# Turning softmax probabilities with a transposing DMA of two float16 parts, in a cross-attention and feed-forward kernel

## What is computed

```python
def block(x, ctx, pos, mask, Wq, Wk, Wv, Wo, kernel, bias):
    h = layernorm(x)
    q = rope((h @ Wq).reshape(32, 64, 32, 128), pos)
    k = rope((ctx @ Wk).reshape(32, 64, 8, 128), pos)
    v = (ctx @ Wv).reshape(32, 64, 8, 128)
    scores = q . k / sqrt(128)            # each k, v head serves 4 q heads
    scores = where(mask == 0, -1e9, scores)
    p = softmax(scores)
    x = x + (p @ v).reshape(32, 64, 4096) @ Wo
    f = layernorm(x)
    return x + f @ mxfp4(kernel) + bias   # kernel rounded to 4-bit values and back
```

## Time and profile before

| | |
|---|---|
| median of three runs | 1138.07 us (1137.52 to 1138.55) |
| span of the profiled execution | 1136.2 us (its own time beside the span is not recorded; the median stands 1.9 us above the span) |
| PE busy | 1126.4 us, 99% |
| DVE, ACT, POOL busy | 810.1, 769.0, 629.6 us |
| DMA | 65.6 MB, mean 58 GB/s |

### The profile page before, as it was taken

The page is one execution under the profiler, slowest core; times in us unless marked ns, Lnnn a source line. Parts: engine busy times, 40 slices in busy tenths (PEclk is TensorE's granted clock), DMA queues, the critical chain, the costliest instruction groups (busy, mean ns, idle before and its releaser), DMA issues.

```text
span 1136.2 us, 19698 instructions
## 1 busy us (share of the span) xinstructions
PE 1126.4 (99%) x6315; PEld 971.5 (86%) x6326; DVE 810.1 (71%) x1753; ACT 769.0 (68%) x2306; POOL 629.6 (55%) x518
## 2 busy tenths in 40 slices
PE   7999999999999999999999999999999999999998
PEld 6888888888888888888888788888888888888886
DVE  7877777777777777688788756656566665656698
ACT  7866676566676766688766566676766677666763
POOL 7854645365554655569666556545654446545433
PEclk9999999999999999999999999999999999999999
DMA  8311211112111111224124421110201112020001
GB/s 260 86 34 43 75 39 46 33 43 66 35 51 33 61 39 37 93 71 142 48 68 111 116 75 43 38 48 20 83 10 29 48 38 65 11 73 20 1 7 69
DMA packets 60196, 65.57 MB, mean 58 GB/s; under 512 B 17216, under 2 KB 36032, under 8 KB 60096
## 3 DMA queue, kind: packets, MB, share of 16 engines
q1 hardware_dynamic: 59184, 61.96, 18.3%
q0 software_dynamic: 768, 2.10, 0.6%
q10 hardware_dynamic: 144, 0.26, 0.1%
HBM read 58.01 MB, written 4.19 MB: 55 GB/s over the span
## 4 chain that ended last, share of the span: by engine, by line
PE 98%; DMA 1%; DVE 0%; POOL 0%; issue 0%; DVEq 0%
PE proj L539 15%; PE proj L540 15%; PE proj L541 15%; PE pS L671 9%; PE pO L725 9%; PE pO L726 9%; PE pO L727 9%; PE pV L703 3%; PE pV L704 3%; PE pO L735 3%; PE pT L686 3%; PE pO L738 1%; PE proj L602 1%; PE proj L595 1%; PE proj L553 1%; DMA t<-table,tiny 1%
## 5 line engine op out<-in xcount | busy, mean ns | idle before, releaser
L915 ACT CAST PS<-pT 64x256 fp32r<-64x256 f32 x256 | 93.8, 367 | 296.9 <-PE pV L704 293.5
L1436 POOL TENSOR_TENSOR t<-t,SIN 128x512 f32<-128x512 f32 x124 | 159.7, 1288 | 185.9 <-ACT t L924 185.5
L539 PE MATMUL proj<-XH,QH 128*128 128x512 f32 x500 | 195.7, 391 | 0.0
L541 PE MATMUL proj<-XH,QL 128*128 128x512 f32 x500 | 194.8, 390 | 0.0
L540 PE MATMUL proj<-XL,QH 128*128 128x512 f32 x500 | 194.7, 389 | 0.0
L725 PE MATMUL pO<-OH,AH 128*128 128x512 f32 x432 | 171.6, 397 | 0.0
L726 PE MATMUL pO<-OL,AH 128*128 128x512 f32 x432 | 169.2, 392 | 0.0
L727 PE MATMUL pO<-OH,AL 128*128 128x512 f32 x432 | 168.5, 390 | 0.0
L1440 POOL TENSOR_TENSOR qT<-qT,t 128x512 f32<-128x512 f32 x124 | 159.8, 1289 | 9.7
L1156 DVE TENSOR_TENSOR qT<-proj,COS 128x512 f32<-128x512 f32 x128 | 88.4, 690 | 95.1 <-PE proj L541 55.5
L1002 ACT ACTIVATE pS<-pS,tiny 128x64 f32<-128x64 f32 x504 | 140.7, 279 | 7.7 <-DVE tiny L1339 3.6
(11 more groups left out here) (216 smaller groups left out, 2581.4 us busy)
## 6 DMA issues: line engine op xcount, KB each, us to landing
QR<-wq SPq DMA_DIRECT2D x64, 256.0 KB, 2.6
OR<-wo SPq DMA_DIRECT2D x62, 256.0 KB, 3.2
CR<-ctxT SPq DMA_DIRECT2D x16, 256.0 KB, 5.1
KR<-wk SPq DMA_DIRECT2D x16, 256.0 KB, 2.6
UR<-wv SPq DMA_DIRECT2D x16, 256.0 KB, 3.9
acc<-x SPq DMA_DIRECT2D x15, 256.0 KB, 3.8
out<-acc SPq DMA_DIRECT2D x15, 256.0 KB, 2.3
rawx<-x SPq DMA_DIRECT2D x8, 256.0 KB, 2.9
```

The lines of the kernel that those rows point to most:

```text
L539: pe.matmul(dst, lh, rh, start=k == 0, stop=False)
L541: made = pe.matmul(dst, ll, rh, start=False, stop=k == last)
L1436: pool.tensor_tensor(t[:, :], t[:, :], SIN[:, 512 * (s % 2):512 * (s % 2) + 512], ALU.mult).then_inc(g_qs, 1)
```

## The change

p is turned by the DMA engines. DVE scales p by 2^14 as well and writes it into PSUM (`sm` is now the lower half of bank pT). ACT casts it to float16 into P16, each 64-column block written twice side by side (the high part, for both halves of the partitions), at the end of its step. DVE writes the rest as float16 into P16's second half, each block once, beside zeros set at the start. SP starts one transposing DMA of the 128x1024 tile into PT16, one step later. One more step on, at the head of their steps, ACT casts the four high blocks back to the matmul format in PS with the scale 2^-14, and POOL does the same with the four low blocks. `values` reads both from PS, in the same number of matmuls and columns. PE's `turn_p` is gone. POOL's ring for its own DMAs is made smaller (4096).

```diff
+P_SCALE = 2.0 ** 14
-        VS, PS = sb("VS", [128, 2, 8, 256], F32R), sb("PS", [128, 2, 256], F32R)
+        VS, PS = sb("VS", [128, 2, 8, 256], F32R), sb("PS", [128, 8, 128], F32R)
-        PL = sb("PL", [128, 2, 256], F32R)
-        sm = sb("sm", [128, 256], F32)
+        P16, PT16 = sb("P16", [128, 1024], FP16), sb("PT16", [128, 8, 128], FP16)
+        sm = pT[:, 0:256]
 SP, after the weight loads of step n, for m = n - 6:
+            def turn_p(m):
+                if m:
+                    sp.wait_ge(a_ps, m)
+                    sp.wait_ge(g_ps, m)
+                sp.wait_ge(a_ph, m + 1)
+                sp.wait_ge(v_pl, m + 1)
+                sp.dma_start(PT16[:, :, :], P16[:, :], transpose=True).then_inc(d_pt, 16)
 PE:
-            def turn_p(m):
-                pe.wait_ge(v_pn, m + 1)
...
-                for hp in range(2):
-                    made = pe.transpose(pT[:, 128 * hp:128 * hp + 128], sm[:, 128 * hp:128 * hp + 128],
-                                        ident[:, :])
-                made.then_inc(e_pt, 1)
             def values(m):
-                pe.wait_ge(v_pl, 2 * m + 2)
-                pe.wait_ge(a_px, 2 * m + 2)
+                pe.wait_ge(a_ps, m + 1)
+                pe.wait_ge(g_ps, m + 1)
...
-                    pe.matmul(pV[:, b], VS[:, b, j, c], PS[:, b, :], start=True, stop=False)
-                    made = pe.matmul(pV[:, b], VS[:, b, j, c], PL[:, b, :], start=False, stop=True)
+                    pe.matmul(dst, VS[:, b, j, c], PS[:, b:4:2], start=True, stop=False)
+                    made = pe.matmul(dst, VS[:, b, j, c], PS[:, 4 + b::2], start=False, stop=True)
 ACT, p_high(m) at the end of step m + 5 and p_turned(m) first in step m + 7:
             def p_high(m):
-                act.wait_ge(e_pt, m + 1)
-                if m:
-                    act.wait_ge(e_pv, m)
-                for i in range(2):
-                    act.copy(PS[ROWS[i], i, :], pT[ROWS[i], 0:256]).then_inc(a_ph, 1)
+                act.wait_ge(v_pn, m + 1)
+                if m:
+                    act.wait_ge(d_pt, 16 * m)
+                act.activation(P16[:, 0:512].rearrange("p (a d k) -> p a d k", a=4, d=2),
+                               sm.rearrange("p (a k) -> p a k", a=4).unsqueeze(2).broadcast_to([128, 4, 2, 64]),
+                               ACT.Copy).then_inc(a_ph, 1)
+            def p_turned(m):
+                act.wait_ge(d_pt, 16 * m + 16)
+                if m:
+                    act.wait_ge(e_pv, m)
+                act.activation(PS[:, 0:4], PT16[:, 0:4], ACT.Copy, scale=1.0 / P_SCALE).then_inc(a_ps, 1)
-                        act.copy(PS[ROWS[1 - i], i, :], PS[ROWS[i], i, :].bitcast(F32)).then_inc(a_px, 1)
 DVE, p_low(m) in step m + 6 right after the sum of the output projection:
-                dve.tensor_tensor(sm.rearrange("p (a k) -> p a k", a=4), v4, rinv.unsqueeze(2).broadcast_to([128, 4, 64]),
-                                  ALU.mult).then_inc(v_pn, 1)
+                dve.scalar_tensor_tensor(sm.rearrange("p (a k) -> p a k", a=4), v4, P_SCALE,
+                                         rinv.unsqueeze(2).broadcast_to([128, 4, 64]), ALU.mult,
+                                         ALU.mult).then_inc(v_pn, 1)
+            def p_low(m):
+                dve.wait_ge(a_ph, m + 1)
+                v = sm.rearrange("p (h i k) -> p h i k", h=2, i=2)
+                high = P16[:, 0:512].rearrange("p (h i d k) -> p h i d k", h=2, i=2, d=2)[:, :, :, 0, :]
+                dve.tensor_tensor(P16[:, 512:1024].rearrange("p (h u k) -> p h u k", h=2, u=4)[:, :, 0:4:3, :],
+                                  v, high, ALU.subtract).then_inc(v_pl, 1)
-                    for i in range(2):
-                        dve.wait_ge(a_ph, 2 * (m - 1) + i + 1)
-                        dve.tensor_tensor(PL[ROWS[i], i, :], pT[ROWS[i], 0:256], PS[ROWS[i], i, :].bitcast(F32),
-                                          ALU.subtract).then_inc(v_pl, 1)
 POOL, first in step m + 7:
+            def p_turned(m):
+                pool.wait_ge(d_pt, 16 * m + 16)
+                if m:
+                    pool.wait_ge(e_pv, m)
+                pool.tensor_scalar(PS[:, 4:8], PT16[:, 4:8], 1.0 / P_SCALE, None, ALU.mult).then_inc(g_ps, 1)
-    nc = _bacc.Bacc("TRN2", target_bir_lowering=False, num_devices=1)
+    nc = _bacc.Bacc("TRN2", target_bir_lowering=False, num_devices=1, dynamic_dma_scratch_size=4096)
```

More of the change, by code:

```diff
@@ L87 @@
 PART = [range(0, 1), range(1, 4), range(4, 8)] + [range(k, k + 1) for k in range(8, QUANT)]
-def quant_steps(n):
-    parts = quant_parts(n)
-    return sum(QUANT * i + PART[c].stop for i, c in parts[-1:]) if parts and parts[-1][1] < len(PART) else (
-        QUANT * parts[-1][0] + QUANT if parts else 0)
 def quant_parts(n):
@@ L494, in _ @@
                     load_stream(streamed(n))
+                if 0 <= n - 6 < PAIRS:
+                    turn_p(n - 6)
                 if n + 1 in X_AT and X_AT[n + 1] >= 8:
@@ L694, in values @@
                 c = slice(128 * (G % 2), 128 * (G % 2) + 128)
-                pe.wait_ge(v_pl, 2 * m + 2)
-                if not m:
-                    pe.wait_ge(v_const, 3)
-                pe.wait_ge(a_px, 2 * m + 2)
+                pe.wait_ge(a_ps, m + 1)
+                pe.wait_ge(g_ps, m + 1)
                 pe.wait_ge(v_vl, v_count(s - 2 * (G % 2), p))
@@ L963, in _ @@
                 m = n - 5
+                if 0 <= m - 2 < PAIRS:
+                    p_turned(m - 2)
                 if 0 <= n - 1 < PAIRS and n - 1 not in ALONE:
@@ L1227, in _ @@
             dve.memset(mhalf, -0.5).then_inc(v_const, 1)
-            for i in range(2):
-                dve.memset(PL[ROWS[1 - i], i, :].bitcast(F32), 0.0).then_inc(v_const, 1)
+            dve.memset(P16[:, 512:1024].bitcast(F32), 0.0).then_inc(v_const, 1)
             statistics("x", 0)
@@ L1284, in _ @@
                         last_sums()
+                if 0 <= m - 1 < PAIRS:
+                    p_low(m - 1)
                 if n in X_AT and X_AT[n] >= 8:
@@ L1356, in _ @@
                     normalise("f", FFN_AT[n])
-                if 0 <= m - 1 < PAIRS:
-                    for i in range(2):
-                        dve.wait_ge(a_ph, 2 * (m - 1) + i + 1)
-                        dve.tensor_tensor(PL[ROWS[i], i, :], pT[ROWS[i], 0:256], PS[ROWS[i], i, :].bitcast(F32),
-                                          ALU.subtract).then_inc(v_pl, 1)
                 if 0 <= m - 2 < PAIRS and n > PAIRS + 1:
@@ L1470, in _ @@
             for n in range(OPENED, END):
+                if 0 <= n - 7 < PAIRS:
+                    p_turned(n - 7)
                 if is_last(n):
```

29 lines of the change are left out of this document (12 added, 17 removed).

## The result

The changed kernel takes **1162.15 us** (median of four runs, 1161.32 to 1162.75) against 1138.07 us before (1137.52 to 1138.55 in four runs): a ratio of **1.0211, 95% interval 1.0199 to 1.0224**. It is 24 us slower, where 3.6 us faster was forecast. The profiled execution has a span of 1159.4 us and a time of 1161.32 us, 1.9 us above its span, as was assumed.

A forecast was written before the change was run, and what follows sets the result against it. PE's instruction stream, 99% busy, was taken to bound the kernel. From 1138.07 us, -29.4 + 1.0 (ACT and DVE at the start) + 9.3 + 4.5 + 11.0 = -3.6 us gave 1134.5 us, range 1121 to 1149.

The forecast's parts named there:

- 128 x 0.23: PE, all pairs: removing two transposes per pair frees 0.23 us each time, 29.4 us in all.
- the slot doesn't close: Rival, PE held by something under the transposes: no gain from their removal; chance 1%.
- GpSimd's queue: POOL's new low-part cast makes values wait in steps 7 to 9, 61 to 66 and other crowded steps: 9.3 us.
- One input instead of two puts it between; I take 0.9 us: POOL's low-part cast of 128x512: priced between 0.56 and 1.30 us, taken as 0.9 us.
- the upper end of 1.30: POOL's cast: upper end of its price, from POOL's two-input operation of 512 columns, 1.30 us.
- The push: POOL's column moved by the cast against the values' start: 9.3 us at 0.9 us a cast, 20 at 1.3.
- GpSimd bounds (slower): Rival: POOL's cast costs 1.3 us, values wait in a step of every eight, total 1145.2 us; chance 20%.
- The feed-forward tiles: Steps 70 to 76: SP issues the p turn ahead of the split turn, making PE late by 4.5 us.
- the p turn waits for DVE's low part: SP in the feed-forward steps: this wait delays the split turn, about 2.0 us in step 76, 1.5 in 75.
- The end: From step 128: p turn behind a store, then the whole loop; gaps 2.8, 3.9, 2.8, plus 1.5: 11.0 us.
- the likeliest case: Whole kernel: 1134.5 us, its own range 1129 to 1141; chance 50%.
- The turn itself: Transposing DMA per pair: 1.24 us of SP's queue, landing after 3.1 us, 4.6 at worst; hidden in the steady stretch.

The follow-up runs named there:

- e5: Kernel before with both transposes left out from pair 9 on (119 pairs), p not turned; 1119.89 us, ratio 0.984.
- e8: Changed kernel with GpSimd casting 320 columns of the turned p instead of 512, ScalarE 704 instead of 512; 1151.63 us, ratio 1.0127.
- e3: Changed kernel with the feed-forward tiles' split turn issued ahead of the p turn on SP; 1149.45 us, ratio 1.0096.
- e7: Changed kernel with two buffers PT16 for the turned p, so a turn waits for the casts of pair m - 2; 1157.51 us, ratio 1.0169.
- e1: Changed kernel with ScalarE casting all eight blocks of the turned p in one instruction, GpSimd none; 1140.74 us, ratio 1.0025.
- e2: Changed kernel with SP's feed-forward stores at the end put one step later, behind the next p turn; 1152.69 us, ratio 1.013.
- e10: Changed kernel with both casts of the turned p as plain copies, the factor 2^-14 moved into the split of v; 1143.63 us, ratio 1.005.
- e11: Changed kernel with e10, e2 and e3 together; 1124.94 us, ratio 0.9883.
- e6: Changed kernel with e1, e2 and e3 together; 1121.36 us, ratio 0.9853.

## Why the prediction was wrong

Step by step, in spans. The sum forecast was -3.6 us and +23.2 came: 26.8 us apart.

- **Removed from PE: -29.4 forecast, -21.8 measured (7.6 us of the miss).** The first step that failed is "128 x 0.23": the distance from the transposes' first load to the values' first load was taken as what the values would move up. Without the transposes the values' load stands 0.06 us behind where the transposes' stood. The trace of before could not show that the load of another kind would start as early; the estimate should have had a lower end there, and had only the rival that the slot doesn't close, at 1%. e5, with nothing else changed, has the same 0.17 us. The warning against taking the 273 to 276 ns of one transpose as its price was right, and it did not go far enough.
- **GpSimd's queue, the start and steps 128 to 130: 11.8 forecast (9.3 + 1.0 + 1.5), 20.7 measured (8.9 us of the miss).** The failed step is "One input instead of two puts it between; I take 0.9 us". The real cast, 1.49 us, lies above the upper end of 1.30, so the bound was no bound: a row of another operation does not cap this one. The places were right: 9.8 us in steps 60 to 66 where 5.4 were forecast, 4.3 at the start where 2.7 + 1.0 were, and small losses elsewhere. The push itself was good: e8, with 1.01 us, has 8.0 us in steps 60 to 66 where 5.4 were forecast for 0.9, and without the slow clock of its step 65 it would have 5.3. So the failed term is the 0.9 us and not the room in POOL's queue; of the changed kernel's 20.7 us, 1.7 are clock in step 65. The condition of the rival "GpSimd bounds (slower)" came, but not its price, 1145.2 for 1.3 us, nor its mark: no step in every eight stalled, but one in sixteen (33, 49, 81, 97, 113) by 0.6 us.
- **The feed-forward tiles: 4.5 forecast, 13.0 measured (8.5 us of the miss).** The mechanism, SP's split turn behind its p turn, was right, and e3 shows that it is all. The failed step is "the p turn waits for DVE's low part": the diff has two more waits in `turn_p`, for the casts of the pair before, and they were passed over. e7 shows 5.6 us by them, 1.8 of it through the clock. Steps 70 and 74, forecast at 0.2 to 0.5 us, took 4.6 and 4.1, with PE waiting 2.41 and 2.30 of them and the slow clock behind making the rest. 75 and 76 took 1.8 each, as forecast (1.5 and 2.0). With neither the buffer's wait nor a slow stretch, e1 has 6.0 us here, near the 4.5.
- **The end: 9.5 forecast (11.0 less the 1.5 of steps 128 to 130), 11.3 measured.** Held, in part by luck. The store, the loop and the gaps are as described, and e2 removes all of it. But the gaps sum to 7.9 us of waiting (3.03, 3.40 and 1.49, forecast in the order 2.8, 3.9, 2.8, 9.5 in all), and 3.2 us of clock not granted came on top, with a granted clock of 0.71 in the 5 us behind the first gap and 0.70 behind the second.
- **The clock: nothing in the sum, 8.4 us measured.** The failed step is a term left out. It lies inside the three terms above (1.7, 3.5 and 3.2 us) and so is no further part of the miss, but nearly a third of it. The prediction had it in the GpSimd rival only, at some 3 us for one slow stretch at the end. That price is right (2.9 us between e10 and e11 in step 65); but there were several such stretches, and the likeliest case, which forecast three gaps of 2 to 4 us, had none. The other three executions of the changed kernel were granted 0.990 instead of 0.993, so they lost more to it.
- **The turn itself.** Right: 3.1 us to landing in the median, 5.1 at worst, in 128 turns. The figure of the Trainium skill ("VectorE: DVE Perf Modes", The three transpose paths), 1309 ns a block, is far from what eight blocks at once take here, as the eight split turns had said. ScalarE's two casts at 0.60 and 0.62 us and DVE's low part at 0.42 us were as forecast.
- **769 ns.** The Trainium skill ("GPSIMD Engine Reference", 3.1) gives this for 512 elements as a best case. It lies between the two forms measured here, 0.61 us for a copy and 1.49 us for a multiplication by a constant; the one figure fits neither.

7.6 + 8.9 + 8.5 + 1.8 = 26.8 us. The range of 1121 to 1149 missed because all four terms erred in the same direction, and it was built from one bad term at a time. The cause of the time is shown: e6 takes back 39 of the 45.0 us with three moves, each tried alone before.

## What to carry to other kernels

When work leaves the engine that bounds, read every wait that the new work puts into the queues of DMAs, also those that only protect a buffer: a cast that is late on GpSimd reached, by one buffer and one queue, a matmul with other data. Put a transfer that somebody needs at once ahead of one with slack, and a store behind both; here that was worth 22 us without any work removed. And price a new operation in its exact form: the same cast took 0.61 us as a copy and 1.49 us with a factor in it, and a factor that is a power of two can be moved onto an instruction that is there anyway (in e10 DVE's half of v's split stayed at 0.42 us and ACT's went from 0.37 to 0.38). Charge a gap of the bounding engine more than its length: a slow stretch behind one was worth up to 2.9 us here.

## What had not been expected of the hardware

- GpSimd: `tensor_scalar` with a multiplication over 128x512 takes 1491 ns, from float16 or float32; the plain copy to the same output takes 611 ns. At 320 columns 1011 ns, at 256 columns 849 ns. It is also longer than its `tensor_tensor` on 512 columns (about 1290 ns).
- TensorE: two transposes of 128x128 between scores and values hold back what follows by 0.17 us a pair, by the steady steps of the changed kernel and of e5 alike, though the loads that they occupy span 0.23 us and one is on record with 273 ns.
- TensorE's clock: behind a gap of 2.41 us the granted clock read 0.52 from 600.90 to 603.80 and 1.00 after that; with filler in the gap it stayed at 1.00. Behind a gap of 2.80 us in step 7 it stayed at 1.00 as well, and behind the same 2.55 us in step 65 it read 0.50 in e10 and 1.00 in e11, 2.9 us apart in that step. Two executions of nearly the same kernel can differ by this alone.
- The transposing DMA: 1.24 us of SP's queue and 3.1 us to landing for 128x1024 float16, unchanged at 128 of them and with the DMA queue's share at 35.9% instead of 18.3%.
